# Attention features built in transposed form, with powers of the charge stacked by on-chip moves

## The chip, the cores and the metric

The kernel runs on one core of one Trainium2 chip. The metric is the device time of one execution in microseconds (us); the median over several runs is compared. The engines are called here as in the profile: PE (TensorE matmul), PEld (its weight load), DVE (VectorE), ACT (ScalarE), POOL (GpSimd) and SP (SyncE, which only issues DMAs here). Each engine works through its own instructions in program order and waits on semaphores for the others.

## The reference, cut to what matters

The input is x of 32 sequences, 512 tokens, 256 features, all in fp32. A block of attention with a kernel feature map is followed by a block that routes tokens to 64 slots. Only the feature map matters here:

```python
q = jnp.tanh(x @ W_charge.T + b_charge)[..., 0]
phi_c = mags * q[..., None] ** jnp.arange(ORDER + 1)          # 5 powers, 0 to 4
shell = x @ W_shell.T + b_shell
shell = shell / jnp.maximum(jnp.linalg.norm(shell, axis=-1, keepdims=True), 1e-12)
proj = shell @ omega.T + rff_bias
phi_s = jnp.concatenate([jnp.cos(proj), jnp.sin(proj)], axis=-1) * rff_scale   # 64
tp = (phi_c[..., :, None] * phi_s[..., None, :]).reshape(b, n, -1)             # 320
phi = tp @ W_combine.T                                                         # 64
logits = jnp.einsum('bnd,bmd->bnm', phi, phi) * T / temp      # then causal softmax, V, W_out
# second block: h = gelu(ctx @ w1.T + b1); route logits; top 8 of 64 slots; softmax weights alpha;
# slot_input = alpha^T x; GRU over slots; out = alpha @ (slots @ wv.T + bv) @ wo.T + bo
```

## The kernel before, in words

Everything is done for pairs of sequences, 16 pairs. The main loop makes 19 passes (`it` from 0 to 18), and in a pass four pairs are at work at different stages: `f = it` (layer norm, projection and features), `m = it - 1` (logits, softmax, values), `g = it - 2` (hidden layer, routing, gather) and `o = it - 3` (slot update and output). A step whose pair lies outside 0 to 15 does nothing. On each engine the steps of a pass are written out by hand in one fixed order, so an engine that waits in one step holds up every later step of its list, whichever pair it belongs to. A steady pass takes 47.3 us.

The features of pair f: `proj` on PE makes, per 128 tokens, a row VS of 354 numbers, with the values, the shell (256 to 319), the charge (320) and the angle (321 to 352). `charge` (L575, ACT) takes the tanh of 8 numbers per partition. GpSimd squares the shell (`square`, L1096), VectorE sums, GpSimd takes the inverse root (`rnorm`, L1101, L1103) and the powers of q (`powers`, L1109, L1111), VectorE computes the angles (`phase`, `turns`, `unwind`, `clamp`, L766 to L794), ACT the sine (`sine`, L583), and GpSimd multiplies the 64 sines with four powers (`feats`, L1120, two instructions of 128x1024) into `tp`, tokens on partitions. PE then turns `tp` into feature-major form in six steps of four 128x128 transposes (`tp_t`, line 228 as all transposes), ACT copies each result out of PSUM (`feats_t`, L595), and `phi` (L279) contracts the 320 features in three steps (128, 128 and 64 rows) for each of the two sequences. VectorE scales phi into QF and KF (`qk_full`, L799, L800), ACT rounds them (`qk_high`), GpSimd takes the rest (`qk_low`, L1127, L1129), and SP moves them to both halves of the partitions (`qk_moves`) for the logits of the next pass.

Three other steps stand in the same lists and matter below. On GpSimd, behind `feats`: `sv_low` (L1166), `shift` (L1136, the routing logits of pair g minus their maximum, four instructions), `pick` (L1144), then `ln_norm(it + 1, 0)`, `alpha`, `lm_norm(m, 0)`, `ln_norm(it + 1, 1)` (the last writes xn for the second sequence of the next pass, L1068), `qk_low` and `lm_norm(m, 1)`. On ACT: `expo(m, 5)`, then `route_exp(g, 0)` and `route_exp(g, 1)` (L649, which wait for `shift` of their sequence), then `probs_t(m, 4)` (L623), which writes the operand of PE's `values(m, 4)` (L322). On PE: PSUM banks come from three rings (T for transposes, L for logits, G for the rest), and a step waits until its bank has been emptied.

Of the kernel before, what the change touches and what calls it, by code (L numbers as in the profile page):

```python
# [5 lines left out]
B, N, D = 32, 512, 256  # L6
# [69 lines left out]
xnT_t xnT xl vs_mm vs q1 sq n2 n2m rn q2 q4 p1 p2 p3 trig sin tp  # L76
tpT_t tpT phi QF KF Qh Kh Ql Kl qk
lg_mm nmax E ET_t ET av_mm rinv av
xmT_t xmT h_mm h rt_mm lg m8 mr dm ex am0 as0 as1 am gi_mm rw0 rw gin gi_t gi
rz_mm grz srz gx_mm rhn gn nn hd hz sn aT_t aT aTl as sv_mm sv SVh SVl of_mm fin  # L80
""".split()

def build(nc, a, out):
    ctx = ExitStack()
    with ctx:
# [79 lines left out]
        def tpT(d, j):  # L165
            return xmT[:, d, j, :] if j < 2 else tpT2[:, d, :]
# [36 lines left out]
        QF, KF, QR, KR = xmT[:, 0, 0, :], xmT[:, 0, 1, :], xmT[:, 1, 0, :], xmT[:, 1, 1, :]  # L203
# [10 lines left out]
        def _(e):  # L214
# [41 lines left out]
            @live  # L256
            def tp_t(k, d, j):
                b = 2 * k + d
                w = 128 if j < 2 else 64
                tv = tp[:, d, :, :, :].rearrange("p t m r -> p t (m r)")  # L260
                p, before = T.take(s["tpT"], 3 * b + j + 1)
                at["tp", b, j] = p
                if before:
                    e.wait_ge(*before)
                if j == 0:
                    e.wait_ge(s["tp"], b + 1)
                transposes(p, [tv[:, t, j * 128:j * 128 + w] for t in range(4)]).then_inc(s["tpT_t"], 1)

            @live
            def phi(k):  # L270
                p, before = G.take(s["KF"], k + 1)
                at["phi", k] = p
                if before:
                    e.wait_ge(*before)
                e.wait_ge(s["tpT"], 6 * k + 6)
                for j in range(3):
                    w = 128 if j < 2 else 64
                    for d in range(2):
                        ins = e.matmul(p[64 * d:64 * d + C, :], wc[0:w, j, :], tpT(d, j)[0:w, :],  # L279
                                       start=j == 0, stop=j == 2)  # L280
                ins.then_inc(s["phi"], 1)
# [194 lines left out]
            for it in range(NP + 3):  # L476
# [17 lines left out]
                logits(m, 2)  # L494
                e_t(m, 0)
# [10 lines left out]
                route(g, 1)  # L506
                values(m, 1)
                if it == 0:
                    e.wait_ge(s["soft"], SOFT)
                tp_t(f, 0, 0)  # L510
                logits(m, 5)
                e_t(m, 3); values(m, 2)
                tp_t(f, 0, 1)
# [16 lines left out]
        def _(e):  # L530
# [39 lines left out]
            def charge(k):  # L570
                VP = VS[:, (2 * k) % 4:(2 * k) % 4 + 2, :, :]
                e.wait_ge(s["vs"], 8 * k + 8)
                if k:
                    e.wait_ge(s["tp"], 2 * k)
                e.activation(qq[:, :, :, 0:1], VP[:, :, :, 320:321], ACT.Tanh).then_inc(s["q1"], 1)  # L575

            @live
            def sine(k):
                e.wait_ge(s["trig"], k + 1)
                if k:  # L580
                    e.wait_ge(s["tp"], 2 * k)
                    e.wait_ge(s["tpT_t"], 6 * k)
                e.activation(tp[:, :, :, 0, :], tg[:, :, :, :], ACT.Sin).then_inc(s["sin"], 1)  # L583

            @live
            def feats_t(k, d, j):
                b = 2 * k + d
                w = 128 if j < 2 else 64
                e.wait_ge(s["tpT_t"], 3 * b + j + 1)
                if d == 0 and j == 0 and k:  # L590
                    e.wait_ge(s["phi"], k)
                    e.wait_ge(s["qk"], 192 * k)
                    if k >= 2:
                        e.wait_ge(s["h_mm"], 2 * (k - 2) + 2)
                e.activation(tpT(d, j)[0:w, :], at["tp", b, j][0:w, :], ACT.Copy).then_inc(s["tpT"], 1)  # L595
# [30 lines left out]
            def xm_copy(k, d, c):  # L626
                b = 2 * k + d
                e.wait_ge(s["xmT_t"], 2 * b + c + 1)
                if d == 0 and c == 0:
                    later = min(k + 1, NP - 1)  # L630
                    e.wait_ge(s["qk"], 192 * (later + 1))
# [50 lines left out]
            for it in range(NP + 3):  # L682
# [14 lines left out]
                expo(m, 1); probs_t(m, 0)  # L697
# [9 lines left out]
                feats_t(f, 0, 0)  # L707
                expo(m, 4); probs_t(m, 3)
                feats_t(f, 0, 1)
# [3 lines left out]
                feats_t(f, 0, 2); feats_t(f, 1, 0); feats_t(f, 1, 1)  # L713
                expo(m, 7); probs_t(m, 6)
                feats_t(f, 1, 2)
# [4 lines left out]
        def _(e):  # L720
# [238 lines left out]
            def attention_setup():  # L959
                e.wait_ge(s["w"], 16 * 6)  # L960
                e.wait_ge(s["pool_setup"], POOL_TEMP)
                e.reciprocal(t8(8), t8(4)).then_inc(s["soft"], 1)
                for c in range(2):
                    e.tensor_scalar(wc[:, c, :], wc[:, c, :], wcs[:, c:c + 1], None, ALU.mult).then_inc(s["soft"], 1)
                e.tensor_scalar(wc[0:64, 2, :], wc[0:64, 2, :], wcs[0:64, 2:3], None, ALU.mult).then_inc(s["soft"], 1)
# [90 lines left out]
        def _(e):  # L1056
# [50 lines left out]
            def powers(k):  # L1107
                e.wait_ge(s["q1"], k + 1)
                e.tensor_tensor(qq[:, :, :, 1:2], qq[:, :, :, 0:1], qq[:, :, :, 0:1], ALU.mult).then_inc(s["q2"], 1)  # L1109
                e.wait_ge(s["q2"], k + 1)  # L1110
                e.tensor_tensor(qq[:, :, :, 2:4], qq[:, :, :, 0:2], qq[:, :, :, 1:2].broadcast_to([128, 2, 4, 2]),  # L1111
                                ALU.mult).then_inc(s["q4"], 1)

            @live
            def feats(k, d):
                b = 2 * k + d
                if d == 0:
                    e.wait_ge(s["sin"], k + 1)
                    e.wait_ge(s["q4"], k + 1)
# [264 lines left out]
```

## Time and profile before

| what | value |
|---|---|
| median of 3 runs | 843.04 us (842.33 to 845.62) |
| the profiled execution's own time | 842.98 us |
| its span, first to last instruction | 841.2 us |
| PE busy | 759.1 us, 90% |
| DVE, POOL, ACT busy | 624.9, 514.3, 414.0 us |
| mean granted TensorE clock | 0.973 of full |
| bytes moved by DMA | 80.33 MB |

A busy share is an average over the span. With one fixed list per engine, what counts is which wait ends last ahead of an instruction; the views in order of time show that in square brackets as [idle before <-releaser].

### The profile page before, as it was taken

Reading aid. Unit: us, or ns where it says so; the run is one execution under the profiler, and the core shown is the slowest. Engines: PE = TensorE matmul, PEld = TensorE weight load, DVE = VectorE, ACT = ScalarE, POOL = GpSimd, SP = SyncE. Lnnn points to the kernel's source line nnn. Section 1 sums busy time; section 2 is a strip of 40 time slices with the busy share of each in tenths; the row PEclk is TensorE's granted clock in tenths of the full one; section 3 lists DMA queues with packets and bytes.
Section 4 is the critical chain, followed back from the end, with each engine's and each line's share of the span. In section 5 each row is a group of like instructions: output and inputs, shape, how many; then the busy total and the mean of one; then the engine's idle time right before and its main releaser. Section 6 shows DMA issues by size and latency. Waiting matters only on the chain.

```text
span 841.2 us, 15464 instructions
## 1 busy us (share of the span) xinstructions
PE 759.1 (90%) x4704; PEld 609.2 (72%) x4704; DVE 624.9 (74%) x2054; ACT 414.0 (49%) x886; POOL 514.3 (61%) x873
## 2 busy tenths in 40 slices
PE   4847999999999999999999999999999999998962
PEld 3835776878787777878787777878787777877752
DVE  2646677787969788787969788787969788775642
ACT  0334565554728274554728274554728274556421
POOL 5273758494766749394766749394766759372520
PEclk9879999999999999999999999999999999999976
DMA  8004131424262432525262432524262433325133
GB/s 280 3 6 120 39 88 39 112 66 138 51 176 51 125 92 61 149 63 142 51 174 53 125 93 66 144 65 138 52 175 51 119 97 68 94 61 132 60 99 101
DMA packets 69785, 80.33 MB, mean 96 GB/s; under 512 B 9990, under 2 KB 52552, under 8 KB 69704
## 3 DMA queue, kind: packets, MB, share of 16 engines
q1 hardware_dynamic: 65440, 76.15, 34.7%
q10 hardware_dynamic: 4264, 3.20, 1.2%
q8 instruction: 39, 0.64, 0.3%
q14 instruction: 42, 0.34, 0.1%
HBM read 20.60 MB, written 16.78 MB: 44 GB/s over the span
## 4 chain that ended last, share of the span: by engine, by line
PE 64%; DVE 13%; POOL 10%; issue 5%; SPq 3%; ACT 3%; DMA 2%; DVEq 0%; POOLq 0%; ACTq 0%
PE ps L322 14%; PE ps L252 14%; PE ps L228 11%; PE ps L279 5%; PE ps L388 3%; PE ps L373 3%; POOL n L1103 3%; PE ps L359 3%; PE ps L445 2%; DVE xl L738 2%; PE ps L446 2%; PE ps L430 2%; DVE tg L766 2%; POOL xn L1068 2%; DVE tg L770 1%
## 5 line engine op out<-in xcount | busy, mean ns | idle before, releaser
L322 PE MATMUL ps<-VS,ET 128*128 128x256 f32 x640 | 159.6, 384 | 4.9 <-ACT ET L623 4.8
L322 PEld LDWEIGHTS ps<-VS,ET 128*128 128x128 f32 x640 | 112.9, 190 | 28.4 <-issue 17.4
L1120 POOL TENSOR_TENSOR tp<-tp,qq 128x1024 f32<-128x1024 f32 x32 | 60.2, 1903 | 100.4 <-ACT tp L583 100.4
L749 DVE TENSOR_TENSOR VS<-ps,biasM 128x354 f32<-128x354 f32 x128 | 67.2, 525 | 49.6 <-PE ps L252 49.5
L634 ACT ACTIVATE xmT<-ps 128x512 f32<-128x512 f32 x64 | 35.9, 586 | 109.4 <-PE ps L228 99.1
L252 PE MATMUL ps<-W1h,xh 128*128 128x354 f32 x256 | 86.6, 338 | 0.1
L252 PE MATMUL ps<-W1l,xh 128*128 128x354 f32 x256 | 82.6, 323 | 0.0
L252 PE MATMUL ps<-W1h,xl 128*128 128x354 f32 x256 | 82.5, 322 | 0.0
L822 DVE SCALAR_TENSOR_TENSOR X<-ps,rinv,X 128x256 f32<-128x256 f32 x128 | 61.9, 484 | 25.0 <-PE ps L322 20.0
L1096 POOL TENSOR_TENSOR tg<-VS 128x256 f32<-128x256 f32 x32 | 19.6, 613 | 93.7 <-DVE VS L749 89.6
L567 ACT ACTIVATE xh<-ps 128x512 fp32r<-128x512 f32 x64 | 35.3, 598 | 82.4 <-PE ps L228 82.3
L1068 POOL TENSOR_SCALAR xm<-X,rs 128x256 f32<-128x256 f32 x128 | 69.4, 556 | 3.3
L1068 POOL TENSOR_SCALAR xn<-X,rs 128x256 f32<-128x256 f32 x128 | 69.3, 555 | 3.3
L1061 POOL TENSOR_TENSOR rs<-rs,half 128x4 f32<-128x4 f32 x64 | 66.1, 1033 | 5.3
L613 ACT ACTIVATE E<-ps,nmax 128x128 f32<-128x128 f32 (+3 forms) x128 | 67.2, 525 | 3.8 <-DVE nmax L809 3.4
L228 PE MATMUL ps<-ident,tp 128*128 128x128 f32 (+1 forms) x384 | 54.2, 281 | 12.1 <-POOL tp L1120 11.3
L809 DVE TENSOR_REDUCE nmax<-ps 128x1 f32<-128x128 f32 (+3 forms) x128 | 60.8, 476 | 5.4 <-PE ps L299 5.3
L228 PEld LDWEIGHTS ps<-ident,tp 128*128 128x128 f32 (+1 forms) x384 | 44.6, 134 | 21.8 <-issue 18.1
L295 PE MATMUL ps<-KH,QS 128*128 128x256 f32 (+2 forms) x128 | 55.0, 430 | 5.7 <-ACT E L613 3.5
L347 PE MATMUL ps<-xmT,w1a 128*128 128x512 f32 x128 | 58.6, 599 | 0.1
L623 ACT ACTIVATE ET<-ps 128x128 f32<-128x128 f32 (+3 forms) x128 | 55.0, 430 | 4.8 <-PE ps L228 3.7
L228 PE MATMUL ps<-ident,E 128*128 128x128 f32 x320 | 56.8, 276 | 0.1
(173 smaller groups left out, 1966.7 us busy)
## 6 DMA issues: line engine op xcount, KB each, us to landing
X<-in_x SPq DMA_DIRECT2D x32, 512.0 KB, 4.2
out_x<-X SPq DMA_DIRECT2D x32, 512.0 KB, 4.1
QS<-xmT SPq DMA_DIRECT2D x64, 128.0 KB, 2.3
KH<-xmT SPq DMA_DIRECT2D x64, 128.0 KB, 2.3
KL<-xmT SPq DMA_DIRECT2D x64, 128.0 KB, 2.4
AS<-grz SPq DMA_DIRECT2D x32, 128.0 KB, 2.3
AS<-aTl SPq DMA_DIRECT2D x32, 128.0 KB, 2.4
SVS<-gn SPq DMA_DIRECT2D x64, 64.0 KB, 2.1
```

The lines of the kernel that those rows point to most:

```text
L228: ins = e.transpose(p[0:m, j * 128:j * 128 + 128], block_in, ident[:, :])
L252: ins = e.matmul(p[:, 0:FEATS], x[:, d, c, t * 128:t * 128 + 128], w[:, c, :], start=j == 0, stop=j == 5)
L295: e.matmul(p[:, 0:wide], QS[:, d, i * 128:w], KH[:, d, 0:wide], start=True, stop=False, skip_group_check=True)
L322: ins = e.matmul(p[:, 0:D], ET[:, r % 2, j * 128:j * 128 + 128], VS[:, (2 * k + d) % 4, j, 0:256], start=j == 0, stop=j == i)
L347: ins = e.matmul(p[:, :], w1a[:, c, :], xmT[:, d, c, :], start=c == 0, stop=c == 1)
L613: e.activation(E[:, r % 3, 0:w], at["lg", r][:, 0:w], ACT.Exp, bias=nmax[:, r % 8:r % 8 + 1], accum_out=rsum[:, r % 8:r % 8 + 1]).then_inc ...
L749: e.tensor_tensor(VS[:, b % 4, t, :], at["vs", b, t][:, 0:FEATS], biasM[:, :], ALU.add).then_inc(s["vs"], 1)
L809: e.tensor_reduce(nmax[:, r % 8:r % 8 + 1], at["lg", r][:, 0:w], AX.X, ALU.max, negate=True).then_inc(s["nmax"], 1)
L822: e.scalar_tensor_tensor(X[:, b % NX, i, :], at["av", r][:, 0:D], rinv[:, r % 8:r % 8 + 1], X[:, b % NX, i, :], ALU.mult, ALU.add).then_in ...
L1061: e.tensor_tensor(r[:, d, 0, :], r[:, d, 1, :], half[:, 0:4], ALU.pow).then_inc(s[tag + "_r"], 1)
L1068: ins = e.tensor_scalar(dst[:, t, :], x[:, t, :], r[:, d, 0, t:t + 1], r[:, d, 2, t:t + 1], ALU.mult, ALU.add)
L1120: e.tensor_tensor(tp[:, d, :, 1:5, :], tp[:, d, :, 0:1, :].broadcast_to([128, 4, 4, 64]), qq[:, d, :, :].unsqueeze(3).broadcast_to([128, 4 ...
```

## The change

It changes how the 320 features per token are built. Before, the powers multiply the sines with tokens on partitions, and the product of 320 columns is transposed. After, the charge and the 64 sines are each transposed once, and the multiplications run on the transposed tiles.

- ACT: `charge` now writes the tanh 64 times over (QN, 128x512). PE transposes it (`q_t`, four transposes, behind `logits(m, 2)`), and ACT copies it to QB (`q_copy`). `sine` writes PS, in the order that lets four transposes (`z_t`, behind `route(g, 1)`) turn both sequences at once: Z[:, 0] has sequence 0 on partitions 0 to 63 and sequence 1 on 64 to 127 (`z_copy` on ACT, where `feats_t(f, 0, 0)` was).
- GpSimd: `powers` and `feats` go. In the place of `feats` (behind `slot_change`) stands a new `powers`: Z[i+1] = Z[i] * QB for i from 0 to 3, each 128x512, each waiting for the one before, the first for `z_copy` and `q_copy`.
- SP: `z_moves`, eight DMAs of 128 KB per pair, put Z[0] and Z[1], and Z[2] and Z[3], one above the other in xmT for each sequence. They stand between the first four and the last four slot moves.
- PE: the six `tp_t` go. `phi` keeps twelve matmul records; its third step reads Z[4] in place and uses a copy of the weights on the same half of the partitions. It waits for the four multiplications and the eight moves.
- QF, KF, QR and KR now lie in Z, so `xm_copy` of the next pass waits for phi instead of the moves of Q and K.

```diff
             @live
-            def tp_t(k, d, j):
-                ...
-                transposes(p, [tv[:, t, j * 128:j * 128 + w] for t in range(4)]).then_inc(s["tpT_t"], 1)
+            def q_t(k):
+                ...
+                e.wait_ge(s["q1"], k + 1)
+                transposes(p, [QN[:, t, :, :].rearrange("p b r -> p (b r)") for t in range(4)]).then_inc(s["q_t"], 1)
+            def z_t(k):
+                ...
+                e.wait_ge(s["sin"], k + 1)
+                transposes(p, [PS[:, t, :, :].rearrange("p b r -> p (b r)") for t in range(4)]).then_inc(s["z_t"], 1)
             def phi(k):
-                e.wait_ge(s["tpT"], 6 * k + 6)
-                for j in range(3):
-                    w = 128 if j < 2 else 64
+                e.wait_ge(s["zm"], 4 * k + 4)
+                e.wait_ge(s["zs"], 128 * (k + 1))
+                for j in range(2):
                     for d in range(2):
+                        e.matmul(p[own(d), :], wc[:, j, :], stacked(d, j), start=j == 0, stop=False)
+                for d in range(2):
+                    ins = e.matmul(p[own(d), :], wc[own(d), 2, :], Z[own(d), 4, :], start=False, stop=True)
 # PE's list
                 logits(m, 2)
+                q_t(f)
                 e_t(m, 0)
 ...
                 route(g, 1)
+                z_t(f)
                 values(m, 1)
-                tp_t(f, 0, 0)
 ...
-                tp_t(f, 0, 2); tp_t(f, 1, 0); tp_t(f, 1, 1)
                 values(m, 4)
 # ACT
-                e.activation(qq[:, :, :, 0:1], VP[:, :, :, 320:321], ACT.Tanh).then_inc(s["q1"], 1)
+                e.activation(QN[:, :, :, :], VP.rearrange("p b t a -> p t b a").broadcast_to([128, 4, 2, 64]),
+                             ACT.Tanh).then_inc(s["q1"], 1)
+            def q_copy(k):
+                e.wait_ge(s["q_t"], k + 1)
+                ...
+                e.activation(QB[:, :], at["q", k][:, :], ACT.Copy).then_inc(s["qb"], 1)
+            def z_copy(k):
+                e.wait_ge(s["z_t"], k + 1)
+                ...
+                e.activation(Z[:, 0, :], at["z", k][:, :], ACT.Copy).then_inc(s["zc"], 1)
 # ACT's list
-                expo(m, 1); probs_t(m, 0)
+                expo(m, 1); q_copy(f); probs_t(m, 0)
 ...
                 probs_t(m, 2)
-                feats_t(f, 0, 0)
+                z_copy(f)
                 expo(m, 4); probs_t(m, 3)
-                feats_t(f, 0, 1)
                 expo(m, 5)
                 route_exp(g, 0); route_exp(g, 1)
                 probs_t(m, 4); expo(m, 6); probs_t(m, 5)
-                feats_t(f, 0, 2); feats_t(f, 1, 0); feats_t(f, 1, 1)
 # POOL
             def powers(k):
-                ...
-            def feats(k, d):
-                ...
+                e.wait_ge(s["zc"], k + 1)
+                e.wait_ge(s["qb"], k + 1)
+                for i in range(4):
+                    e.tensor_tensor(Z[:, i + 1, :], Z[:, i, :], QB[:, :], ALU.mult).then_inc(s["zm"], 1)
+                    if i < 3:
+                        e.wait_ge(s["zm"], 4 * k + i + 1)
 # POOL's list
-                rnorm(f); powers(f)
+                rnorm(f)
                 slot_change(o)
-                feats(f, 0); feats(f, 1)
+                powers(f)
                 sv_low(o)
                 shift(g, 0); shift(g, 1)
 # SP
+            def z_moves(k):
+                ...
+                e.wait_ge(s["zc"], k + 1)
+                for i in range(4):
+                    if i:
+                        e.wait_ge(s["zm"], 4 * k + i)
+                    for d in range(2):
+                        e.dma_start(stacked(d, i // 2)[own(i % 2), :], Z[own(d), i, :]).then_inc(s["zs"], 16)
 # SP's list
                 alpha_moves(o)
                 slot_moves(o)
+                z_moves(it)
+                slot_rest_moves(o)
                 qk_moves(it)
```

## Rows read from the trace of the kernel before

**Rows 1.** The page: busy time of each engine, and shares of the chain of work

```profile
PE 759.1 (90%) x4704; PEld 609.2 (72%) x4704; DVE 624.9 (74%) x2054; ACT 414.0 (49%) x886; POOL 514.3 (61%) x873
...
PE 64%; DVE 13%; POOL 10%; issue 5%; SPq 3%; ACT 3%; DMA 2%; DVEq 0%; POOLq 0%; ACTq 0%
```

**Rows 2.** PE's instructions in order of time (start us, us, what), one steady pass

```profile
401.20 1.10 PE L430 MATMUL ps<-Wvo,SN 128*128 128x256 f32 x4 [0.37 <-DVE SN L908]
...
404.15 1.08 PE L322 MATMUL ps<-VS,ET 128*128 128x256 f32 x4
405.29 0.63 PE L228 MATMUL ps<-ident,tp 128*128 128x128 f32 x4
...
411.28 1.47 PE L228 MATMUL ps<-ident,tp 128*64 128x128 f32 x12
412.59 0.60 PE L322 MATMUL ps<-VS,ET 128*128 128x256 f32 x2
...
415.59 1.94 PE L279 MATMUL ps<-xmT,wc 128*64 128x512 f32 x8 [0.34 <-ACT tpT L595]
...
425.58 1.47 PE L228 MATMUL ps<-ident,xn 128*128 128x128 f32 x12
427.59 0.44 PE L228 MATMUL ps<-ident,GIN 128*128 128x128 f32 x2 [0.54 <-DVE xl L738]
```

**Rows 3.** ScalarE's instructions in order of time, the same pass

```profile
395.09 0.70 ACT L668 ACTIVATE gn<-gn,bihn 128x128 f32<-128x128 f32 x2 [0.69 <-DVE gn L897]
...
402.54 0.63 ACT L583 ACTIVATE tp<-tg 128x512 f32<-128x512 f32 x1
...
406.11 0.59 ACT L595 ACTIVATE xmT<-ps 128x512 f32<-128x512 f32 x1
...
409.38 1.29 ACT L649 ACTIVATE lg<-lg 128x512 f32<-128x512 f32 x2
410.58 0.26 ACT L623 ACTIVATE ET<-ps 128x128 f32<-128x128 f32 x1
```

**Rows 4.** GpSimd's instructions in order of time, the same pass

```profile
395.86 0.82 POOL L1160 TENSOR_TENSOR gt<-S,gn 128x256 f32<-128x256 f32 x1
403.24 3.76 POOL L1120 TENSOR_TENSOR tp<-tp,qq 128x1024 f32<-128x1024 f32 x2 [6.57 <-ACT tp L583]
406.97 0.73 POOL L1166 TENSOR_TENSOR gt<-gt,gn 128x256 fp32r<-128x256 f32 x1
407.65 2.36 POOL L1136 TENSOR_TENSOR lg<-lg,m 128x256 f32<-128x256 f32 x4
...
423.44 2.17 POOL L1068 TENSOR_SCALAR xn<-X,rs 128x256 f32<-128x256 f32 x4
```

**Rows 5.** GpSimd's groups by line and shape: count, busy us, mean ns

```profile
L1127 POOL TENSOR_TENSOR xmT<-xmT 128x512 fp32r<-128x512 f32 x16 | 20.5, 1279 | 0.7 <-ACT xmT L600 0.7
```

**Rows 6.** VectorE's instructions in order of time, the same pass

```profile
395.33 0.29 DVE L766 TENSOR_TENSOR tg<-VS,n 128x128 f32<-128x128 f32 x1 [0.28 <-POOL n L1103]
...
396.00 0.82 DVE L766 TENSOR_TENSOR tg<-VS,n 128x128 f32<-128x128 f32 x1
```

**Rows 7.** The DMA queue of SyncE: four issues in order of time

```profile
405.86 2.38 SPq L1300 DMA_DIRECT2D SVS<-gn  x4
```

**Rows 8.** The page's DMA issues: count, KB each, us from issue to landing

```profile
KH<-xmT SPq DMA_DIRECT2D x64, 128.0 KB, 2.3
```

**Rows 9.** PE's instructions in order of time, first and second pass

```profile
61.73 0.63 PE L228 MATMUL ps<-ident,xn 128*128 128x128 f32 x4 [1.38 <-POOL xn L1068]
...
81.07 1.56 PE L322 MATMUL ps<-VS,ET 128*128 128x256 f32 x4 [4.83 <-ACT ET L623]
```

**Rows 10.** GpSimd's instructions in order of time, first pass

```profile
49.19 3.76 POOL L1120 TENSOR_TENSOR tp<-tp,qq 128x1024 f32<-128x1024 f32 x2 [4.54 <-ACT tp L583]
```

**Rows 11.** PE by stretch of the second pass: length, busy us, granted clock

```profile
81.50:82.00 0.50, 0.50 (x4) 0.58 0.00 0
...
85.00:85.50 0.50, 0.50 (x5) 1.00 0.00 0
```

More of the change, by code:

```diff
@@ L75 @@
 ln_s ln_a ln_v ln_r ln_m ln_m2 ln_n lm_s lm_a lm_v lm_r lm_m lm_m2 lm_n
[L76 to L77 removed]
+xnT_t xnT xl vs_mm vs  sq n2 n2m rn p1 p2 p3 trig sin
+  phi QF KF Qh Kh Ql Kl qk
 lg_mm nmax E ET_t ET av_mm rinv av
@@ L80 @@
 rz_mm grz srz gx_mm rhn gn nn hd hz sn aT_t aT aTl as sv_mm sv SVh SVl of_mm fin
+q1 q_t qb z_t zc zm zs
 """.split()
@@ L163, in build, with stacked @@
         aTl = sb("aTl", [128, N], FR)
-        def tpT(d, j):
-            return xmT[:, d, j, :] if j < 2 else tpT2[:, d, :]
+        def stacked(d, j):
+            return xmT[:, d, j, :]
         wv_n = X[:, 4, 0:2, :]
@@ L579, in sine @@
                 e.wait_ge(s["trig"], k + 1)
-                if k:
[L581 to L591, printed above, removed]
+                e.activation(PS[:, :, :, :].rearrange("p t b r -> p b t r"), tg[:, :, :, :],
+                             ACT.Sin).then_inc(s["sin"], 1)
+            @live
+            def z_copy(k):
+                e.wait_ge(s["z_t"], k + 1)
+                if k:
                     e.wait_ge(s["qk"], 192 * k)
-                    if k >= 2:
-                        e.wait_ge(s["h_mm"], 2 * (k - 2) + 2)
-                e.activation(tpT(d, j)[0:w, :], at["tp", b, j][0:w, :], ACT.Copy).then_inc(s["tpT"], 1)
+                e.activation(Z[:, 0, :], at["z", k][:, :], ACT.Copy).then_inc(s["zc"], 1)
             @live
@@ L630, in xm_copy @@
                     later = min(k + 1, NP - 1)
-                    e.wait_ge(s["qk"], 192 * (later + 1))
+                    e.wait_ge(s["phi"], later + 1)
                     if k:
@@ L763, in phase @@
                 e.wait_ge(s["rn"], k + 1)
+                if k:
+                    e.wait_ge(s["z_t"], k)
                 for d in range(2):
@@ L1198, in following @@
                     e.wait_ge(s["pool_setup"], n)
-                e.wait_ge(s["w"], 16 * 6)
-                for m in range(5):
-                    following(e.memset(wcs[64 * (m % 2):64 * (m % 2) + 64, m // 2:m // 2 + 1], MAGS[m] * RFF))
+                e.wait_ge(s["w"], 16 * 7)
+                for m in range(4):
+                    following(e.memset(wcs[own(m % 2), m // 2:m // 2 + 1], MAGS[m] * RFF))
+                following(e.memset(wcs[:, 2:3], MAGS[4] * RFF))
                 following(e.tensor_scalar(t8(0), ltb, -1.0, None, ALU.mult))
@@ L1317, in _ @@
             load(wc[:, 0:2, :], a["W_combineT"][0:256, :].rearrange("(c p) n -> p c n", c=2))
-            load(wc[0:64, 2, :], a["W_combineT"][256:320, :])
+            for d in range(2):
+                load(wc[own(d), 2, :], a["W_combineT"][256:320, :])
             load(U[:, :], a["decay"][0, :].partition_broadcast(128))
```

71 lines of the change are left out of this document (30 added, 41 removed).

## The prediction

> **What bounds the kernel now.** I read the page first: PE is busy 90% of the span and holds 64% of the chain of work, while GpSimd is busy 61% [rows 1]. That alone says that PE work taken away is worth its time. But the page is an average, and every engine has one list in fixed order. So I then read one steady pass in order of time on each engine: PE's pass begins at 378.3 us and the next at 425.58 [rows 2], 47.3 us. The reader should see three things. PE hardly waits (0.37 us ahead of the slot values, 0.34 ahead of phi, 0.54 at the head of a pass [rows 2]). ACT runs the routing exponentials of pair g (two, 1.29 us together) straight ahead of the copy that `values(m, 4)` needs [rows 3]. And GpSimd idles 6.57 us for the sine, then runs `feats`, `sv_low` and `shift` with no gap; `shift` ends at 410.01 [rows 4], and the second routing exponential can only begin then. GpSimd's list so stands close behind PE's at this place, with little in reserve.
>
> **The change, part by part (one steady pass).**
>
> *PE work.* Twelve transposes take 412.59 - 411.28 = 1.31 us, 0.11 each [rows 2]. 24 go (2.6 us), 8 come (0.9): 1.7 us saved. phi keeps its twelve records, two at a time on the two halves of the columns as before; I cost it at nothing. The last copy ahead of phi goes too: its four transposes begin phi's wait, and from their end (0.45 us after four other transposes) to phi at 415.59 some 0.5 us are lost, 0.34 of it shown as idle [rows 2]. If nothing else moved, a pass would be 2.1 us shorter.
>
> *ACT ahead of `sine`.* The tanh grows from 8 to 512 numbers; by the 512-wide sine it is 0.63 us in all [rows 3], of which I take +0.4; the copy of q is some 0.5 more (the 512-wide copy is 0.59 [rows 3], and the next instruction overlaps its end). ACT idles 0.69 us ahead of the later tanh [rows 3] and again ahead of `al_high`, so this is mostly absorbed; `logits(m, 2)` on PE comes 0.4 later, and `q_t` adds 0.43. Of this 0.8 the 0.37 us wait for SN [rows 2] is given back: PE reaches the place of `z_t`, 404.15 before, about 0.45 late, at 404.6. The sine ended at 402.54 + 0.63 = 403.2 [rows 3], so `z_t` need not wait and ends at 405.0.
>
> *The start of the multiplications.* `z_copy` stands where the first feature copy stood, 406.11 to 406.70 [rows 3], behind `probs_t(m, 2)`; with the shifts above I take its end as 406.8. GpSimd began `feats` at 403.24 [rows 4], so it now idles 3.6 us longer. Its 128x1 to 128x16 instructions of the old `powers` lay in front of `slot_change`, off this path.
>
> *The length of the multiplications.* The trace has no 128x512 product of this kind. Nearest is L1127, 128x512 with two full operands, 1.28 us [rows 5]; the other side is `feats`, which reads one operand broadcast: 3.76 us for 2048 columns [rows 4], 0.94 per 512. I take 1.28, because Z and QB are both read in full as in L1127, and keep 0.94 for the range. Four with three hand-overs of 0.08: 5.35 us, from 406.85 to 412.2, against 407.0 before. The Trainium skill (GPSIMD Engine Reference, 3.1 Elementwise) gives 4497 ns for a two-input fp32 instruction of 2048 elements; an estimate from that page is 1.12 us per 512, which would take 0.6 us off each pass.
>
> *What is queued behind them.* `sv_low` (0.73) and four `shift` (2.36) [rows 4]: `shift` ends at 415.3, 5.3 late. ACT has long finished `expo(m, 5)` and stands in `route_exp`; 0.6 after 415.3 comes `probs_t(m, 4)`, 415.9 against 410.58 [rows 3], and `values(m, 4)` can begin at 416.25 against 412.59 [rows 2], 3.7 late. PE is there where the twelve transposes began, 411.28 [rows 2], less one earlier set of four (0.35) and plus the 0.45 above: 411.4. It idles 4.9 us. Behind this, `tp_t(f, 1, 2)` and the lost half microsecond are gone (-0.9), and `expo(m, 6)`, which waited in the same queue, costs some 0.2: phi begins 2.9 us late. The 2.1 us saved are already in this.
>
> *The moves.* Four issues take 2.38 us [rows 7], a landing 2.3 us [rows 8]. The pair for Z[3] is issued behind the third multiplication (410.9), and behind the slot moves and the six earlier ones, until 413.2 at the latest, and has landed by 415.5, ahead of phi at 418.5: nothing. The last four slot moves come behind them and land by 418; they are needed at the output matmuls, which come behind phi. The later release of xmT by phi instead of the moves of Q and K is no wait either way here.
>
> *The next pass.* From `shift` to the end of `ln_norm(it + 1, 1)`, 425.61 [rows 4], GpSimd has no slack, so that ends at 430.9. PE wants it 0.9 us after the start of a pass: 425.58 + 2.9 + 0.9 = 429.4. It waits 1.5, of which the waits that stood behind (0.54 [rows 2] and more) absorb 1.0: +0.5. A pass is 3.4 us longer, the clock aside.
>
> *The clock.* In the second pass PE idles 4.83 us ahead of 81.07 [rows 9]. The granted clock then falls to 0.50 within 81.5 to 82.0 and is back at 1.00 at 85.0 [rows 11]: 3.2 us at 1.2 instead of 2.4 GHz, so up to 1.6 us of PE's work lost. The new gap of 4.9 us is as long and comes in each pass. I take the fall in each: +1.6, phi 4.5 late in all. PE then reaches the next pass late enough (431.0) not to wait for GpSimd, so the 0.5 falls away: +4.5 a pass. The Trainium skill (TensorE: Matmul & The Clock Gate, HAM oscillation) says that a wait repeated in every tile can put the engine back to half clock in every tile; by it the sum stays as it is, and the trace agrees with its one gap of this length.
>
> *The ends.* Pass 0 has nothing to hide behind: `feats` began at 49.19 [rows 10]; `z_t` and `z_copy` take until 50.7, and the products until 56.1 instead of 53.0 (49.19 + 3.76), and PE already waits there for xn (1.38 us ahead of 61.73 [rows 9]): +3.1. Pass 1 has no routing, so nothing stands between the products and the normalisation: between a full saving (-2.1) and the cost of pass 0 (+3.1) I take +0.4. Passes 2 to 14 have the whole effect, 13 x 4.5 = 58.5; pass 15 the stall, +4.5. Passes 16 to 18 have no features: nothing. Sum 66.5. Against the profiled execution's own 842.98 us (median 843.04, the same to 0.1) that is 909.5 us; I say 909.
>
> **The rivals.**
>
> *The clock holds.* Steady passes at +3.4: 3.1 + 0.4 + 13 x 3.4 + 2.9 = 50.6, 894 us. For it: one gap is thin evidence.
>
> *Cheap multiplications.* At 0.94 each, everything behind is 1.3 us earlier, the gap is 3.6 us, and the clock may hold: a pass is +2.1, the first +1.8, the last +1.6: 31, 874 us. Against it: L1127.
>
> *GpSimd and VectorE in each other's way.* A VectorE product with two SBUF operands took 0.29 us alone and 0.82 when it met `slot_change` on GpSimd [rows 4, 6]. The Trainium skill (GPSIMD Engine Reference, 1. Specifications) has the two share SBUF interfaces, for such instructions. In the new place, 406.8 to 412.2, VectorE mostly reads PSUM, and `feats` met the like at constant length; if yet each product held up one such operation by 0.5 us on the path, 1 more per pass: 925 us.
>
> *Not slower.* The products are hidden and PE's saving counts: 16 x 2.1 = 34, 809 us. It needs `shift` at most 0.4 us late; the time breaks even at about 2.5 us late, against 5.3. Late start alone is 3.6, so even free multiplications would not quite hide it. Only a much earlier `z_copy` and short products together would.
>
> *Partly.* Some slack that I have missed on ACT or GpSimd halves the stall: 850 to 874 us.
>
> **How the numbers follow.** Forecast with the clock falling, 898 to 920: 0.45. Clock holds, 884 to 898: 0.24. Cheap multiplications: 0.11. Above 920: 0.08. Partly: 0.07. Faster: 0.03; within the bound: 0.02. The range of 8 in 10 leaves out the last four and keeps most of the third: 874 to 921. About 0.5%, 4 us, is what a measurement of this kernel can tell from no change; slower by more 0.95, within 0.02, faster 0.03.
>
> **What would show it.** Right: PE idle 4 to 5 us ahead of `values(m, 4)`, released by ACT's copy (L623 before); ACT idle ahead of `route_exp`, released by GpSimd's `shift`; GpSimd idle about 10 us ahead of the first product, released by `z_copy`; products of 1.2 to 1.3 us; a granted clock that falls once a pass; a steady pass near 51.8 us. Wrong: PE busy over 90% as before, ACT without that idle time, `z_copy` ending at 404, or products under 0.7 us. A pass of 50.7 with the clock at 1.00 would be the first rival; a wait on the moves ahead of phi would show that my cost of nothing for them was wrong.

## The result, and the profile after

The changed kernel takes 920.39 us (918.98 to 921.57, 4 runs) beside 842.68 us for the kernel before: a ratio of 1.0909 [1.0885, 1.0933], slower by 9%. The forecast was 909 us. The page of after (busy time of each engine, the granted clock in 40 slices, the shares of the chain, one row of the DMA issues):

```profile
PE 767.5 (83%) x4448; PEld 602.7 (66%) x4448; DVE 624.4 (68%) x2054; ACT 388.7 (42%) x822; POOL 527.6 (57%) x872
...
PEclk8768998989899998999899899989899898999976
...
PE 51%; POOL 17%; DVE 12%; ACT 9%; issue 7%; SPq 2%; DMA 1%; ACTq 0%; DVEq 0%; POOLq 0%
...
xmT<-Z SPq DMA_DIRECT2D x128, 128.0 KB, 2.3
```

Against [rows 1], PE has 256 instructions fewer (4448 for 4704) and is yet busy 8 us longer; its share of the chain falls from 64 to 51% and GpSimd's rises from 10 to 17%. Work has left PE, and PE has got slower and waits. The rows of a steady pass say where. PE in order of time (start us, us, what, [idle before <-releaser]):

```profile
416.16 1.68 PE L232 MATMUL ps<-ident,xn 128*128 128x128 f32 x12
418.17 0.44 PE L232 MATMUL ps<-ident,GIN 128*128 128x128 f32 x2 [0.33 <-DVE xl L745]
...
442.37 0.61 PE L232 MATMUL ps<-ident,tg 128*128 128x128 f32 x4
...
448.75 0.39 PE L232 MATMUL ps<-ident,E 128*128 128x128 f32 x2
454.27 1.19 PE L333 MATMUL ps<-VS,ET 128*128 128x256 f32 x2 [5.13 <-ACT ET L633]
```

ScalarE in the same pass:

```profile
440.75 0.63 ACT L597 ACTIVATE tg<-tg 128x512 f32<-128x512 f32 x1
...
444.32 0.59 ACT L605 ACTIVATE Z<-ps 128x512 f32<-128x512 f32 x1
...
452.18 0.63 ACT L659 ACTIVATE lg<-lg 128x512 f32<-128x512 f32 x1 [4.49 <-POOL lg L1136]
453.33 0.63 ACT L659 ACTIVATE lg<-lg 128x512 f32<-128x512 f32 x1 [0.53 <-POOL lg L1136]
453.87 0.26 ACT L633 ACTIVATE ET<-ps 128x128 f32<-128x128 f32 x1
```

GpSimd in the same pass:

```profile
445.00 5.31 POOL L1120 TENSOR_TENSOR Z<-Z,QB 128x512 f32<-128x512 f32 x4 [9.77 <-ACT Z L605]
450.26 0.72 POOL L1166 TENSOR_TENSOR gt<-gt,gn 128x256 fp32r<-128x256 f32 x1
450.94 2.35 POOL L1136 TENSOR_TENSOR lg<-lg,m 128x256 f32<-128x256 f32 x4
```

Read backwards, these are the forecast's steps. PE idles 5.13 us ahead of `values(m, 4)`, because ACT's copy comes at 453.87; that stands behind the two routing exponentials, which waited 4.49 and 0.53 us for `shift`; `shift` stands behind the four products, and these began when `z_copy` ended, at 444.9. The transposes of the sines (442.37) did not wait. The pass of [rows 2] began here:

```profile
378.28 1.47 PE L228 MATMUL ps<-ident,xn 128*128 128x128 f32 x12
```

Counted from the start of the pass on PE (416.16 in after, 378.28 before), `shift` ends 5.4 us later than before and `values(m, 4)` begins 3.8 later, where the forecast had 5.3 and 3.7.

The second half of the loss is the clock. PE by stretch (length, busy us and records, granted clock, share of the DMA engines, GB/s), first around the stall of the pass before, then around the one above, then around an earlier one:

```profile
402.00:402.50 0.50, 0.01 (x1) 0.54 0.39 86
402.50:403.00 0.50, 0.50 (x1) 0.50 0.53 119
...
405.00:405.50 0.50, 0.50 (x3) 0.54 0.00 0
405.50:406.00 0.50, 0.50 (x6) 1.00 0.00 0
```

```profile
453.00:453.50 0.50, 0.00 (x0) 0.74 0.41 90
453.50:454.00 0.50, 0.00 (x0) 0.50 0.58 131
...
459.00:460.00 1.00, 1.00 (x4) 0.50 0.00 0
460.00:461.00 1.00, 1.00 (x6) 0.97 0.00 0
```

```profile
239.50:240.00 0.50, 0.00 (x0) 1.00 0.89 201
...
241.50:242.00 0.50, 0.00 (x0) 0.62 0.91 205
...
248.50:249.00 0.50, 0.50 (x5) 1.00 0.00 0
```

The first two times PE has done nothing for 4 to 5 us (since 397.4 and since 449.1) when the clock falls from the level of 2.4 to that of 1.2 GHz; the third time for only 2.1 us (since 239.5). It is back after 3.4 us the first time and after 6.8 us the other two, of which the last spends 3 us in the stall (PE goes on at 244.6). From pass 1 to pass 15 it is low 16 times in after (once in before, [rows 11]): twelve times for about 6.8 us, four times for about 3.4.

From the starts of PE's passes, the profiled executions (921.57 and 842.98 us) differ so:

| part | before | after | difference | forecast |
|---|---|---|---|---|
| up to pass 0 | 20.1 | 20.6 | +0.5 | 0 |
| pass 0 | 39.1 | 43.3 | +4.2 | +3.1 |
| pass 1 | 40.9 | 39.3 | -1.6 | +0.4 |
| pass 2 | 41.5 | 50.2 | +8.7 | +4.5 |
| passes 3 to 14, mean | 47.32 | 52.56 | +5.24, twelve times 62.9 | +4.5, twelve times 54 |
| from pass 15 on | 131.8 | 135.6 | +3.8 | +4.5 |
| sum | | | +78.5 | +66.5 |

### The profile page after: what moved, and what is told of

Its sections match the earlier page's. It is cut to its first block, busy times and chain, and to the rows that moved or that the text cites. A ratio compares the mean times of both kernels' runs of the same rounds, so it can differ in the third digit from the quotient of the medians.

```text
span 919.8 us, 15032 instructions
## 1 busy us (share of the span) xinstructions
PE 767.5 (83%) x4448; PEld 602.7 (66%) x4448; DVE 624.4 (68%) x2054; ACT 388.7 (42%) x822; POOL 527.6 (57%) x872
## 4 chain that ended last, share of the span: by engine, by line
PE 51%; POOL 17%; DVE 12%; ACT 9%; issue 7%; SPq 2%; DMA 1%; ACTq 0%; DVEq 0%; POOLq 0%
PE ps L256 14%; PE ps L333 10%; POOL Z L1120 8%; PE ps L232 7%; PE ps L399 4%; POOL lg L1136 4%; PE ps L289 3%; PE ps L384 3%; DVE tg L779 2%; PE ps L456 2%; ACT L623 2%; DVE xl L745 2%; PE ps L457 2%; PE ps L291 2%; ACT ET L633 1%
## 5 line engine op out<-in xcount | busy, mean ns | idle before, releaser
L333 PE MATMUL ps<-VS,ET 128*128 128x256 f32 x640 | 180.3, 420 | 70.9 <-ACT ET L633 70.9
L333 PEld LDWEIGHTS ps<-VS,ET 128*128 128x128 f32 x640 | 124.3, 210 | 99.4 <-issue 86.2
L1120 POOL TENSOR_TENSOR Z<-Z,QB 128x512 f32<-128x512 f32 x64 | 81.3, 1270 | 156.8 <-ACT Z L605 153.0
L756 DVE TENSOR_TENSOR VS<-ps,biasM 128x354 f32<-128x354 f32 x128 | 67.3, 526 | 51.7 <-PE ps L256 51.5
L633 ACT ACTIVATE ET<-ps 128x128 f32<-128x128 f32 (+3 forms) x128 | 55.5, 434 | 39.2 <-PE ps L232 39.1
L232 PE MATMUL ps<-ident,E 128*128 128x128 f32 x320 | 66.0, 313 | 0.2
L306 PE MATMUL ps<-KH,QS 128*128 128x256 f32 (+2 forms) x128 | 56.9, 444 | 10.1 <-ACT E L623 8.9
L232 PEld LDWEIGHTS ps<-ident,E 128*128 128x128 f32 x320 | 46.9, 169 | 9.3 <-issue 6.4
L842 DVE BATCH_NORM_STATS2 stats<-X 128x6 f32<-128x256 f32 x128 | 52.7, 412 | 0.0
```

Of the source, the lines that this page charges most:

```text
L232: ins = e.transpose(p[0:m, j * 128:j * 128 + 128], block_in, ident[:, :])
L333: ins = e.matmul(p[:, 0:D], ET[:, r % 2, j * 128:j * 128 + 128], VS[:, (2 * k + d) % 4, j, 0:256], start=j == 0, stop=j == i)
L633: e.activation(ET[:, r % 2, 0:w], at["E", r][:, 0:w], ACT.Copy).then_inc(s["ET"], 1)
L756: e.tensor_tensor(VS[:, b % 4, t, :], at["vs", b, t][:, 0:FEATS], biasM[:, :], ALU.add).then_inc(s["vs"], 1)
L1120: e.tensor_tensor(Z[:, i + 1, :], Z[:, i, :], QB[:, :], ALU.mult).then_inc(s["zm"], 1)
```

## The experiments

All are edits of the changed kernel, but for the last. Ratios are to the kernel before on the same chip.

| kernel | us | ratio | steady pass |
|---|---|---|---|
| no moves | 920.80 | 1.0902 [1.0866, 1.0939] | 51.7 to 53.4 |
| half products | 905.34 | 1.0719 [1.0677, 1.0762] | 51.2 |
| routing exponentials later | 907.37 | 1.0743 [1.0647, 1.084] | 48.2 to 56.3 |
| products early | 928.11 | 1.0989 [1.0888, 1.109] | 50.9 to 53.4 |
| filler of 20 matmuls | 945.33 | 1.1198 [1.1171, 1.1226] | 53.6 |
| products after the clamp | 859.44 | 1.0181 [1.0158, 1.0204] | 47.3 to 50.8 |
| normalisation on ACT | 845.82 | 1.0015 [0.9995, 1.0035] | 46.3 |
| filler of 10 matmuls | 903.63 | 1.0712 [1.0692, 1.0731] | 50.8 |
| reordered | 827.80 | 0.9811 [0.9797, 0.9826] | 45.9 |
| before, reordered | 847.69 | 1.0048 [1.003, 1.0065] | 47.3 |

**Do the moves cost anything?**

```diff
-            return xmT[:, d, j, :]
+            return Z[:, 2 * j + d, :]
...
-                e.wait_ge(s["zs"], 128 * (k + 1))
...
-                z_moves(it)
```

> The eight moves per pair are left out and phi reads two tiles of Z in place, so phi is another sum. Theory (the wait on GpSimd's products sets the pass): the moves land before phi asks for them, so the time stays at the changed kernel's 920 us within 3. Rival (the 16.8 MB of added traffic, or SP's 5 us of added issues, cost something): the time falls by more than 5 us.

920.80 us against 920.39: 128 DMA instructions and 16.8 MB gone, and nothing gained. The forecast's price of nothing for the moves holds while the stall is there. It does not hold in pass 0, which takes 41.7 us here and 43.3 in after. Where the stall is gone they do show: three kernels below wait about 0.9 to 1.1 us for them ahead of phi, and in some passes more.

**Does the stall follow the length of the products?**

```diff
+                e.wait_ge(s["qb"], k + 1)
+                if k:
+                    e.wait_ge(s["qk"], 192 * k)
+                for i in range(4):
+                    e.tensor_tensor(Z[:, i + 1, 256:N], QB[:, 256:N], QB[:, 0:256], ALU.mult)
                 e.wait_ge(s["zc"], k + 1)
-                e.wait_ge(s["qb"], k + 1)
...
-                    e.tensor_tensor(Z[:, i + 1, :], Z[:, i, :], QB[:, :], ALU.mult).then_inc(s["zm"], 1)
+                    e.tensor_tensor(Z[:, i + 1, 0:256], Z[:, i, 0:256], QB[:, 0:256], ALU.mult).then_inc(s["zm"], 1)
```

> Half of the columns of each product are computed early, in GpSimd's idle time, from the charge alone (so those columns are not the feature); the products behind the sines are 128x256. Theory: by L1166, 128x256 with two full operands, each is 0.73 instead of 1.28 us, 2.2 us less behind z_copy, and the idle time of PE ahead of values(m, 4) falls from 5.1 to 3 us. If the granted clock still falls: 52.4 - 2.2 = 50.2 a pass, about 889 us. If it holds: some 1.7 less, 48.5 a pass, about 865 us. Rival (length does not matter, only the late start or the moves): 920 us.

PE in order of time in this kernel:

```profile
434.17 1.10 PE L441 MATMUL ps<-Wvo,SN 128*128 128x256 f32 x4 [1.59 <-DVE SN L917]
...
446.88 1.19 PE L333 MATMUL ps<-VS,ET 128*128 128x256 f32 x2 [2.98 <-ACT ET L633]
```

The products behind the copy take 3.15 us instead of 5.31, 2.16 less, and the wait is 2.98 instead of 5.13, 2.15 less: the stall follows their length one to one. But a pass is 51.2 us and not 50.2, and the time 905.34 us and not 889, because there is a new wait of 1.59 us for VectorE, above. I had put the other halves into GpSimd's idle time and counted that as free. The next experiment but one shows the same, larger. Around the stall of 2.98 us the clock still falls, once in each pass from 5 to 15, for 3.4 us.

**Does the stall sit in what is queued behind, or in the products?** The exponentials go behind ScalarE's work for the attention, and VectorE's weight sums go later with them (not shown):

```diff
-                route_exp(g, 0); route_exp(g, 1)
                 probs_t(m, 4); expo(m, 6); probs_t(m, 5)
                 expo(m, 7); probs_t(m, 6)
+                route_exp(g, 0)
                 probs_t(m, 7)
+                route_exp(g, 1)
```

> The two routing exponentials move behind probs_t(m, 6) and probs_t(m, 7) on ACT, and their sums behind attended(m, 4) and (m, 5) on VectorE. Theory: the idle time ahead of values(m, 4) goes, but shift, pick and both layer norms of the next pass still end 5.3 us late on GpSimd, so the wait returns ahead of the transposes of xn for the next pass, some 5 to 6 us long; the pass is 50.5 to 51.5 us and the time 890 to 910 us. Rival (the queue on ACT is the whole cause): PE's saving appears, a pass of 45.2 us and about 812 us.

```profile
411.78 1.09 PE L232 MATMUL ps<-ident,xn 128*128 128x128 f32 x4 [4.47 <-POOL xn L1077]
...
448.31 0.63 PE L232 MATMUL ps<-ident,E 128*128 128x128 f32 x4 [1.11 <-ACT E L623]
449.83 1.94 PE L289 MATMUL ps<-xmT,wc 128*64 128x512 f32 x8 [0.89 <-DMA xmT<-Z]
```

These are the waits of PE over 0.6 us in one pass, in order of time. None stands ahead of `values(m, 4)` any more; it has moved to the head of the pass, 4.47 us for GpSimd's xn, and only 13 us are won. The clock still falls in most passes, and the length of a pass goes up and down, 51.5 us on average. So there are two walls, one behind the other: ACT's order, and GpSimd's chain from the products to `ln_norm(it + 1, 1)`. The second is the one that the forecast's next-pass step priced at 0.5 us, as long as the first stood in front of it.

**Can the products run in GpSimd's idle time?** They take QB in place of the sines, so that they need not wait for `z_copy`; the arithmetic is another, the number and size of the instructions the same. They wait, as `z_copy` does, for the moves of Q and K of the pair before, since these lie in Z:

```diff
-                e.wait_ge(s["zc"], k + 1)
                 e.wait_ge(s["qb"], k + 1)
+                if k:
+                    e.wait_ge(s["qk"], 192 * k)
...
-                    e.tensor_tensor(Z[:, i + 1, :], Z[:, i, :], QB[:, :], ALU.mult).then_inc(s["zm"], 1)
+                    e.tensor_tensor(Z[:, i + 1, :], Z[:, i, :] if i else QB[:, :], QB[:, :], ALU.mult).then_inc(s["zm"], 1)
```

> The four products keep size, number and place in the list, but start from the charge alone and do not wait for z_copy (so the features lack the sines in powers 1 to 4). Theory: they run in GpSimd's idle time, shift ends on time, PE's stall goes, and the saving of 24 - 8 transposes shows: 16 x 2.1 = 34 us under the kernel before, 805 to 818 us, with the clock at 1.00 in steady passes. Rival (the products cost by their length or by contention wherever they run, or the moves do): above 840 us.

928.11 us: more than 100 us above what I expected, and slower than the kernel it came from. My expectation treated 10 us of idle GpSimd as free. VectorE in this kernel, where the angles are made:

```profile
439.02 1.15 DVE L787 TENSOR_SCALAR tg<-tg 128x512 f32<-128x512 f32 x1
440.20 1.38 DVE L789 TENSOR_SCALAR tg<-tg 128x512 f32<-128x512 f32 x1
441.62 1.64 DVE L794 SCALAR_TENSOR_TENSOR tg<-tg 128x512 f32<-128x512 f32 x1
443.29 1.64 DVE L797 SCALAR_TENSOR_TENSOR tg<-tg 128x512 f32<-128x512 f32 x1
```

and in after (the groups of VectorE: busy us, mean ns of one):

```profile
L794 DVE SCALAR_TENSOR_TENSOR tg<-tg 128x512 f32<-128x512 f32 x16 | 11.1, 693 | 0.6
L797 DVE SCALAR_TENSOR_TENSOR tg<-tg 128x512 f32<-128x512 f32 x16 | 11.1, 692 | 0.5
L787 DVE TENSOR_SCALAR tg<-tg 128x512 f32<-128x512 f32 x16 | 6.8, 427 | 0.5
L789 DVE TENSOR_SCALAR tg<-tg 128x512 f32<-128x512 f32 x16 | 6.8, 427 | 0.6
```

GpSimd and PE of the early kernel at that time:

```profile
438.67 1.22 POOL L1121 TENSOR_TENSOR Z<-QB 128x512 f32<-128x512 f32 x1
439.97 4.41 POOL L1121 TENSOR_TENSOR Z<-Z,QB 128x512 f32<-128x512 f32 x3
```

```profile
446.47 2.05 PE L441 MATMUL ps<-Wvo,SN 128*128 128x256 f32 x4 [3.53 <-DVE SN L917]
```

Four instructions of 427 to 693 ns take 1.15 to 1.64 us, one for each product, and the last three products themselves 1.39 us on average instead of 1.27. Each seems to wait out the other engine's instruction. VectorE's busy time grows from 624.4 to 682.8 us, and PE waits 3.53 us for it ahead of the slot values (0.37 in [rows 2]). The clock falls in each pass from 2 to 15 here too, for 3.4 to 10.2 us, though the stall is shorter than in after. The Trainium skill (SBUF — State Buffer, Who interferes with whom) says that VectorE, with two SBUF inputs or in a 2-port mode, and GpSimd exclude each other for a whole instruction; the lengths here agree with it.

**The same, placed after the collision.** As in the kernel just shown, but the products wait for VectorE's `clamp`, its last instruction on the angles (the wait that both have for Q and K is not shown):

```diff
-                e.wait_ge(s["zc"], k + 1)
+                e.wait_ge(s["trig"], k + 1)
...
```

> As the run with early products (they start from the charge alone, so the features lack the sines in powers 1 to 4), but they now wait for VectorE's last step on the angles (L803, the clamp), so they begin about 1 us behind it: 4.5 us ahead of z_copy's end, and behind the VectorE instructions with two SBUF operands that the early products had stretched. Theory (late start and length set the pass, and early products fail only because VectorE and GpSimd hold each other up): shift ends 0.7 us later than in the kernel before, PE's stall ahead of values(m, 4) goes, a pass is 46.2 to 47.0 us and the time 825 to 842 us. Rival (something else in the changed kernel costs the time wherever the products stand): above 880 us.

```profile
413.88 1.04 POOL L1122 TENSOR_TENSOR Z<-QB 128x512 f32<-128x512 f32 x1 [5.36 <-DVE tg L803]
415.00 3.98 POOL L1122 TENSOR_TENSOR Z<-Z,QB 128x512 f32<-128x512 f32 x3
```

```profile
422.97 0.67 PE L333 MATMUL ps<-VS,ET 128*128 128x256 f32 x2 [0.51 <-ACT ET L633]
...
426.75 1.94 PE L289 MATMUL ps<-xmT,wc 128*64 128x512 f32 x8 [0.90 <-DMA xmT<-Z]
```

VectorE's busy time is back at 623.4 us and 859.44 us come out: 69 us less than with products that need not wait those 5.36 us. That settles both points: the late start of the products makes the stall, and in the earlier place it was the meeting with VectorE that took the gain away. It is still above my 825 to 842. The waits that are left (0.51, 0.31, and 0.90 for the moves) eat the 2.1 us of PE's saving in most passes. Three of the steady passes take 50.0 to 50.8 us. In each of them PE waits 2.0 to 2.8 us for the moves, and the clock falls for 3.4 us, beginning in that wait or at most 1 us behind it:

```profile
475.92 2.71 PE L289 MATMUL ps<-xmT,wc 128*64 128x512 f32 x8 [2.76 <-DMA xmT<-Z]
```

In this pass the last two moves landed 4.1 and 4.0 us after their issue, instead of 2.3; the DMA engines were nearly idle for one of these us (busy share 0.07 from 473 to 474), and why is open.

**How much is the clock?** Filler matmuls ahead of `values(m, 4)` keep PE busy through the stall and do nothing else:

```diff
+                if n == 4 and k >= 1:
+                    for j in range(20):
+                        e.matmul(p[:, 0:D], ident[:, :], Wvo[:, 0, :], start=True, stop=True)
```

> In passes 2 to 16, 20 matmuls of 128x256 whose result is overwritten are added ahead of the wait of values(m, 4): about 4.4 us of work inside PE's idle time of 5.1 us. Everything else is the changed kernel. Theory (the fall of the granted clock adds to the wait): the clock stays at 1.00 in the steady passes, a pass is 50.7 instead of 52.4 us, and the time falls from 920 to about 897 us although PE does more. Rival (the wait alone sets the pass, the clock costs nothing): 918 to 923 us.

This filler was mis-sized. Each of these fp32 matmuls shows as two records, so 20 make 40 records and 8.80 us, 3.7 more than the stall. The clock stayed up, but the filler itself was the new bound: 945.33 us instead of the expected 897, and the run does not price the clock. With `range(10)`:

> The filler again with 10 matmuls instead of 20: each ran as two records of 0.22 us, so 20 took 8.8 us and ended 3.6 us behind the operand that values(m, 4) waits for; 10 take 4.4 us and fit into the 5.1 us. In the run with 20 the granted clock stood at 1.00 and a pass was 53.6 us; less the 3.6 that is 50.0. Theory (the fallen clock adds 2 to 2.5 us to a pass of 52.5): a pass of 50.0 to 50.7 and 885 to 898 us. Rival (the clock costs nothing beside the wait): 918 to 923 us.

```profile
409.43 0.63 PE L232 MATMUL ps<-ident,xn 128*128 128x128 f32 x4 [1.39 <-POOL xn L1079]
422.27 0.44 PE L306 MATMUL ps<-KH,QS 128*128 128x384 f32 x1 [0.51 <-ACT E L626]
445.43 0.70 PE L336 MATMUL ps<-VS,ET 128*128 128x256 f32 x2 [0.73 <-ACT ET L636]
460.26 0.63 PE L232 MATMUL ps<-ident,xn 128*128 128x128 f32 x4 [1.41 <-POOL xn L1079]
```

These are all of PE's waits over half a microsecond in one pass, and the first of the next. The filler takes 4.48 us, the clock stays at 1.00 in steady passes (mean 0.966 over the span, 0.915 in after), and the pass is 50.8 us, eleven times in a row (passes 4 to 14). PE is now fast enough to wait 1.4 us for GpSimd's xn, which is what then bounds the pass. The same eleven passes take 52.5 in after, so the clock costs 1.7 us a pass, and 920.39 - 903.63 = 17 us in all. Split by passes of after: the two in which it was low for 3.4 us took 51.7, 0.9 above 50.8; the nine with 6.8 us took 52.7 on average, 1.9 above. These nine are of two kinds. In five the clock fell 2.1 to 2.4 us after PE had stopped, so that 3 us of the low stretch lay in the stall, and the pass took 52.2 to 52.4; in four it fell 4.0 to 4.5 us after, and the pass took 53.1 to 53.4. An estimate from these rows: take half of the time for which PE was busy at the low clock (2.8 to 6.2 us) off a pass, and in all eleven 50.2 to 50.3 us are left.

903.63 us is above the 885 to 898 that I expected. The steady pass accounts for little of that (50.8 us, beside 50.0 to 50.7 expected); pass 3 takes 54.3, with a wait of 3.34 us for xn and one more fall of the clock.

**Can both walls be moved?** The exponentials go later as above, and ScalarE, busy 42% of the span, applies the normalisation of xn in place of GpSimd; the other moves of the text below (`lm_norm`, `z_moves`) are not shown:

```diff
+                ins = e.activation(xn[:, d, t, :], X[:, b % NX, t, :], ACT.Identity,
+                                   bias=rs[:, d, 2, t:t + 1], scale=rs[:, d, 0, t:t + 1])
```

> A version meant to keep the change and lose its cost: the routing exponentials and their sums late as in the earlier run; the layer norm of the next pair is applied by ACT (128x256 with scale and bias per partition) at the end of its list, so GpSimd's four instructions of 0.55 us per sequence go; lm_norm(m, 1) moves into GpSimd's idle time of the next pass, lm_norm(m, 0) behind qk_low; z_moves stand ahead of the slot moves. Theory (after the products, GpSimd's chain up to the xn of the next pass is what bounds a pass): that chain is 8.7 us shorter (4.4 of applying, 4.3 of lm_norm), neither PE's stall ahead of values(m, 4) nor the one ahead of xn is left, and only the landing of the last moves holds up phi by about 1 us: a pass of 45.5 to 46.5 us, 818 to 838 us, faster than the kernel before by 1 to 3%. Rival (the products and moves still end too late, or ACT becomes the bound): 843 us or more.

845.82 us, level with before. The steady pass is 46.3 us, under the 47.3 of before, but the run was above my range. PE waits:

```profile
468.28 0.63 PE L232 MATMUL ps<-ident,E 128*128 128x128 f32 x4 [1.11 <-ACT E L634]
470.04 1.94 PE L289 MATMUL ps<-xmT,wc 128*64 128x512 f32 x8 [1.13 <-DMA xmT<-Z]
```

and the first passes, which have little to hide behind, were longer (pass 0 took 47.6 us against 39.1). The next version mends these: `z_copy` ahead of `probs_t(m, 2)`, VectorE's statistics behind the last `row_max`, the first pass's xn on GpSimd as before, and phi contracting the stack in two parts so that it starts when half the moves have landed:

```diff
-                e.wait_ge(s["zs"], 128 * (k + 1))
+                e.wait_ge(s["zs"], 64 * (k + 1))
...
+                e.wait_ge(s["zs2"], 64 * (k + 1))
```

> The reordered version again, mended where its trace showed waits: the second half of the next pair's statistics goes behind row_max(m, 7) on VectorE (1.1 us of PE's waiting ahead of e_t(m, 7)); z_copy goes ahead of sv_high and probs_t(m, 2); phi takes Z[4] in place second and the tile moved last at the end, with a semaphore of its own for the last four moves; the first pair is normalised by GpSimd as before, and in passes 0 and 1 ACT applies the next norm ahead of qk_high. Theory: steady passes of 45.2 to 45.8 instead of 46.3 (the kernel before: 47.3), 8 us less in the first passes, 818 to 832 us, 1 to 3% faster than the kernel before. Rival (GpSimd's chain or the landing of the moves still bounds the pass): 46.3 us a pass and 836 to 840.

GpSimd's products and all of PE's waits over 0.2 us in one pass:

```profile
448.08 5.33 POOL L1143 TENSOR_TENSOR Z<-Z,QB 128x512 f32<-128x512 f32 x4 [9.09 <-ACT Z L618]
```

```profile
421.96 0.44 PE L232 MATMUL ps<-ident,GIN 128*128 128x128 f32 x2 [0.54 <-DVE xl L764]
...
434.81 0.44 PE L308 MATMUL ps<-KH,QS 128*128 128x384 f32 x1 [0.51 <-ACT E L636]
448.83 1.53 PE L335 MATMUL ps<-VS,ET 128*128 128x256 f32 x6 [0.24 <-ACT ET L646]
```

827.80 us (827.14 to 828.21, 5 runs), 1.9% faster than before. The steady pass of 45.9 us is just above the 45.2 to 45.8 expected. The products are as long as in the changed kernel (5.33 us) and begin nearly as late (28.1 us into the pass, against 28.8), behind 9.09 us of idle time against 9.77. What differs is what stands behind them in the lists, and that GpSimd no longer applies the normalisation. No clock fall is left in passes 2 to 15. What each of the moves is worth alone was not measured.

**Is that gain the reordering's alone?** The same reordering, and ScalarE's part in it, in the kernel before, without the change:

> Control: the kernel before, features built as before with all 24 transposes, but with the same reordering (route_exp and sums late, norm of x applied by ACT, lm_norm moved). Theory (the kernel before is bound by PE's own work, so freeing GpSimd gives it next to nothing, and what the tuned version gains is the transposes): a pass of 46.9 to 47.4 us and 836 to 846 us. Rival (the gain is the reordering's): as fast as the tuned version or faster, below 832 us.

847.69 us, 1.0048 [1.003, 1.0065]: no gain, and somewhat above the range I gave. The pass stays at 47.3 us, because there PE is the bound and had no such waits: it is busy 45.6 of them, as in before. So the 1.4 us a pass between 47.3 and 45.9 come with the change, whose 16 transposes fewer are the only work that it takes from PE; in the pass of 45.9 PE is busy 44.4 us, 1.25 less.

## Why the prediction was right, and where it was mis-sized

The chain of waits came out as forecast, but the number is inside the range by luck: 920.39 lies 0.6 us under its upper end. It also lies in the part above 920 that I gave 0.08, for a cause (products that hold up VectorE) that did not act here.

*PE work: right in kind, rather too large.* 2.1 us were to be saved in a pass without stalls, 1.7 of them by the transposes. The reordered kernel shows 1.4 in its pass, and PE is busy 1.25 us less in it; the half microsecond that I let go ahead of phi came back as waits elsewhere (0.51 and 0.24 us). Over the whole span its PE is busy 742.0 us, 17.1 below [rows 1].

*The start of the multiplications: right.* `z_t` did not wait; the copy ended 0.1 us ahead of the first product, with GpSimd idle for 9.77 us (forecast about 10). The old `powers` instructions that I set aside there are 128x8 and 128x16 in the trace, not 128x1 to 128x16; nothing hangs on it.

*Their length: right.* 5.31 us for four (forecast 5.35), a mean of 1270 ns (forecast 1.28). The bound of 0.94, from a broadcast operand [rows 4], did not apply, and the rival that rested on it falls.

*What is queued behind them: right.* PE's wait was 5.13 us (forecast 4.9), for ACT's copy, behind exponentials that waited for `shift`. The experiment with half products moved it one to one, and the one that placed the same number of products after the clamp took it from 5.13 to 0.51.

*The moves: right in a steady pass.* Nothing, by the run without them. In pass 0, where PE has nothing else to do, it does wait for the last of them ahead of phi, 7.67 us; without them it waits 6.14 there, for the products. I had no term for that: pass 0 came out 1.1 us over the forecast, and is 1.7 shorter without the moves.

*The clock: right in kind, too small.* This is the term of the sum that failed most. The forecast had a held-clock pass of 50.7 us; the filler shows 50.8. It added 1.1 net for a clock that is low for 3.2 us, read from the one fall in the trace of before [rows 11] (its mean of 0.58 in the first stretch puts the fall at 81.6, so 3.4 us), and gave 51.8; the passes of after with a fall of 3.4 us took 51.7. But nine of those eleven passes had 6.8 us, and those took 52.7. One fall in a trace can't show that there is a second length, nor how much of it PE will spend idle. The term was 1.7 instead of 1.1: 0.6 x 12 = 7 of the 12 us by which the sum fell short.

*The ends: pass 2 was wrong by 4.2 us.* I gave it the effect of a steady pass. In it there is no slot work, so that PE's own pass is only 41.5 us, and two low stretches of the clock fall into it, 3.4 us from 108.5 on and 6.8 from 139.2. With the filler it takes 48.2: the second fall is gone there, which is worth some 2 us of the 8.7, but the first is still there. PE also waits 2.97 us for xn at its head, 0.76 in before, and 4.15 us ahead of `values(m, 4)`; these waits and the two falls make up the 8.7 within an estimate from the rows (2.2 + 4.15 + 1.7 + 2.7, less the 2.1 saved). Pass 1 was 2.0 us under the forecast, the part from pass 15 on 0.7 under and the stretch ahead of pass 0 0.5 over.

*The rivals.* "The clock holds" (894 us) falls: it fell in every pass from 2 to 15. "Not slower" falls for this kernel. I had written that only a much earlier `z_copy` and short products together would bring it about; that was wrong, since the reordered kernel does it with long and late products, by other work standing behind them. "GpSimd and VectorE in each other's way" falls for the place in which the change put the products: VectorE's busy time is 624.4 against 624.9 us [rows 1], and the four instructions on the angles are as short. The mechanism is real and large, as the early products show: 58 us of VectorE's time over the kernel, where my forecast priced one meeting of 0.5 us a product, 1 us a pass, from [rows 6]. That was also what failed in my expectation for the early products: I had named this rival and left it out of the next sum.

## What to carry to other kernels

Where each engine has one fixed list, price a change by what stands behind the moved work in its list and by who waits for that: here 1.6 us more of GpSimd work, begun some 4 us later, cost PE 5 us, because two exponentials of another pair stood ahead of a copy that PE needed; putting them behind it, and the normalisation on a less busy engine, turned 9% slower into 2% faster. A stall of some five microseconds in every pass costs more than its length, since the clock falls with it; add that from the rows, and for more than one length of fall. Here stalls of 2 to 3 us did the same in several kernels. Idle time on GpSimd was not free here while VectorE was at work on SBUF in it.

## What the runs showed of the hardware

VectorE's fp32 instructions of 128x512 on SBUF took 0.43 and 0.69 us alone and up to 1.38 and 1.65 beside GpSimd products of the same size, which grew from 1.27 to 1.39 themselves. TensorE's granted clock fell to half around stalls of PE of 5.1 us (after), 3.5 (products early), 3.0 (half products) and 2.0 to 2.8 (after the clamp), from 2.1 us after PE had stopped to 1 us after it had gone on; one stall of 2.0 us passed without a fall (after the clamp, at 332). It came back after about 3.4 or 6.8 us in after, and after up to 10.2 in the kernel with early products, though PE was busy without a gap over 0.2 us from its next instruction on.
